# One maximum over two score banks in place of two over one each, in a decoder layer on one core

## The reference

```
x = layernorm(x + self_attention(x, W))             # one head
x = layernorm(x + cross_attention(x, ctx, ...))     # 16 heads of 64
x = layernorm(x + ffn(x))                           # two products, gates by a top-2 softmax

# cross_attention, for each batch and head:
q = x @ Wq + bq;  k = ctx @ Wk + bk;  v = ctx @ Wv + bv
att = softmax((q * scale) @ k.T)                    # 512 x 512, softmax along the keys
out = concat(att @ v) @ Wo + bo
```

## Time and profile before

| | us |
|---|---|
| median of 3 runs | 1870.48 |
| lowest and highest run | 1868.18, 1873.57 |
| the profiled execution | 1871.99 |
| its span, from the first instruction to the last | 1870.0 |

### The profile page before, as it was taken

One profiled execution on the slowest core, in us unless ns is written; L12 is line 12 of the kernel. 1 busy time (PEld: TensorE's weight loads), 2 busy tenths in 40 slices (PEclk: granted clock), 3 DMA queues, 4 the chain that ended last, 5 costly groups with the idle time before them and its releaser, 6 DMA issues.

```text
span 1870.0 us, 28844 instructions
## 1 busy us (share of the span) xinstructions
PE 1844.4 (99%) x8863; PEld 1521.2 (81%) x8863; DVE 1573.8 (84%) x3386; ACT 1159.4 (62%) x2461; POOL 1042.6 (56%) x1108
## 2 busy tenths in 40 slices
PE   9999999989999999999999999999999999999998
PEld 8888888768888888888888888888888877778887
DVE  6676666789898998989899898998989899968887
ACT  5544554467677676776777777776777777632221
POOL 2322233246667676656656566566656666756773
PEclk9999999999999999999999999999999999999999
DMA  6777787976859786585776858576585866622121
GB/s 225 276 291 278 283 301 274 317 263 189 259 161 312 215 265 221 156 266 152 252 252 193 265 164 270 180 234 219 168 259 173 252 212 184 194 96 91 60 77 68
DMA packets 200920, 400.39 MB, mean 214 GB/s; under 512 B 18112, under 2 KB 82112, under 8 KB 198592
## 3 DMA queue, kind: packets, MB, share of 16 engines
q1 hardware_dynamic: 164720, 329.08, 54.2%
q10 hardware_dynamic: 36048, 69.48, 11.2%
HBM read 211.31 MB, written 88.08 MB: 160 GB/s over the span
## 4 chain that ended last, share of the span: by engine, by line
PE 90%; DVE 5%; DMA 2%; ACT 1%; POOL 1%; issue 1%; ACTq 0%; POOLq 0%; DVEq 0%
PE a_proj L1429 17%; PE a_turned L1429 17%; PE a_av L1468 11%; PE a_score L1442 11%; PE a_proj L48 9%; PE a_proj L1852 5%; PE a_av L1852 5%; PE a_score L48 3%; PE a_av L48 3%; PE a_turned L1452 3%; PE a_proj L1452 3%; DVE all_negmax L1242 1%; DMA all_second_buffer<-x1T_scratch 1%; DVE c_squares L1298 1%; PE a_score L1827 1%; PE a_turned L624 1%
## 5 line engine op out<-in xcount | busy, mean ns | idle before, releaser
L1021 POOL TENSOR_SCALAR c_prob<-c_prob,all_rden 128x512 f32<-128x512 f32 x512 | 352.1, 695 | 496.3 <-DVE all_rden L1248 496.2
L1106 ACT ACTIVATE c_prob<-a_score,all_negmax 128x512 f32<-128x512 f32 x512 | 347.5, 684 | 195.6 <-DVE all_negmax L1242 192.5
L1242 DVE TENSOR_REDUCE all_negmax<-a_score 128x1 f32<-128x512 f32 x512 | 328.8, 684 | 92.3 <-PE a_score L1442 92.2
L1028 POOL TENSOR_TENSOR c_landing<-c_landing,c_flip_hi 128x512 fp32r<-128x512 f32 x250 | 318.4, 1295 | 2.1 <-ACT c_flip_hi L1156 2.0
L1298 DVE STREAM_TRANSPOSE c_squares<-c_prob 128x256 f32<-128x256 f32 x500 | 291.3, 621 | 1.0 <-POOL c_prob L1021 1.0
L1442 PE MATMUL a_score<-c_ks,c_qs 128*128 128x512 f32 x1024 | 277.1, 392 | 9.7 <-ACT c_prob L1106 9.0
L1442 PEld LDWEIGHTS a_score<-c_ks,c_qs 128*128 128x128 f32 x1024 | 190.1, 188 | 56.5 <-issue 8.4
L1468 PE MATMUL a_av<-c_pt,c_vs 128*128 128x512 f32 x512 | 158.3, 391 | 0.0
L343 POOL TENSOR_SCALAR s_prob<-s_prob,s_rden 128x512 f32<-128x512 f32 x32 | 22.2, 694 | 227.5 <-DVE s_rden L515 227.5
L1156 ACT CAST c_flip_hi<-c_landing 128x512 fp32r<-128x512 f32 x250 | 143.3, 625 | 1.4 <-issue 1.3
L1429 PE MATMUL a_proj<-all_third_buffer,all_first_buffer 128*128 128x512 f32 x552 | 138.2, 399 | 0.6 <-DVE c_ks L1267 0.6
(11 more groups left out here) (230 smaller groups left out, 4028.5 us busy)
## 6 DMA issues: line engine op xcount, KB each, us to landing
c_landing<-c_squares SPq DMA_DIRECT2D x500, 128.0 KB, 2.7
c_wk<-wk_scratch SPq DMA_DIRECT2D x64, 512.0 KB, 3.9
c_wq<-wq_scratch SPq DMA_DIRECT2D x64, 512.0 KB, 4.5
c_ks<-c_ks SPq DMA_DIRECT2D x128, 256.0 KB, 3.7
all_first_buffer<-ctxT_scratch ACTq DMA_DIRECT2D x60, 512.0 KB, 8.5
all_second_buffer<-x1T_scratch ACTq DMA_DIRECT2D x60, 512.0 KB, 7.2
ctxT_scratch<-s_csp SPq DMA_DIRECT2D x8, 2048.0 KB, 7.4
c_y<-y_steps_scratch SPq DMA_DIRECT2D x16, 1024.0 KB, 5.6
```

The source lines that it names most:

```text
L1021: nc.gpsimd.tensor_scalar(prob[:, n % 2, i, :], prob[:, n % 2, i, :], rden[:, n % 2, i:i + 1], 1.0, ALU.mult, ALU.mult).then_inc(p_ready, 1)
L1028: nc.gpsimd.tensor_tensor(whole, as_f32(whole), by_square(as_f32(flip_hi_part[:, k, :])), ALU.subtract).then_inc(flip_lo, 1)
L1106: nc.scalar.activation(prob[:, n % 2, i, :], spsum[:, i % 2, :], ACT.Exp, bias=negmax[:, n % 2, i:i + 1], scale=1.0, accum_out=den[:, n % ...
L1242: nc.vector.tensor_reduce(negmax[:, n % 2, i:i + 1], spsum[:, i % 2, :], AX.X, ALU.max, negate=True).then_inc(smax, 1)
```

## The change

The two reductions of a step, each over one bank, become one reduction over both. It waits for the scores of the second tile (the count on `s_mm` is one higher), writes two columns of `negmax`, and raises `smax` by 2. Nothing else is changed: the exponentials, and what they wait for, keep their code.

```diff
-    def max_tile(g, t):
+    def max_tiles(g, t):
+
         n, i = divmod(t, T)
-        dve.wait_ge(s_mm, TILES * g + t + 1)
-        nc.vector.tensor_reduce(negmax[:, n % 2, i:i + 1], spsum[:, i % 2, :], AX.X, ALU.max,
-                                negate=True).then_inc(smax, 1)
+        dve.wait_ge(s_mm, TILES * g + t + 2)
+        nc.vector.tensor_reduce(negmax[:, n % 2, i:i + 2], spsum[:, :, :], AX.X, ALU.max, negate=True).then_inc(smax, 2)
...
-            for tile in tiles:
-                max_tile(*tile)
+            if tiles:
+                max_tiles(*tiles[0])
...
-        max_tile(0, 0)
-        max_tile(0, 1)
+        max_tiles(0, 0)
         recip(0, 0)
         recip(0, 1)
         finish(PROLOGUE[5])
-        max_tile(0, 2)
-        max_tile(0, 3)
+        max_tiles(0, 2)
```

## The result

Over six runs each the kernel after took 1880.36 us (1878.60 to 1883.00) and the kernel before 1872.03 (1868.18 to 1876.14; the three runs shown at first are among them). The ratio is 1.0043 with a 95% interval of 1.0031 to 1.0055, a loss of some 8.1 us where 6.5 were forecast. The profiled execution took 1883.00 us, 2.6 above its median, with a span of 1881.0; that of before took 1871.99.

A forecast was written before the change was run, and what follows sets the result against it. TensorE was taken as the bound; front 2.4, middle 0.7 and last stretch 3.4 made 6.5 us on top of 1871.99, so 1878.5 for the profiled execution and 1877 for the median, range 1872 to 1884.

The forecast's parts named there:

- Front: First group of eight heads in the cross-attention: TensorE's waits for exponentials grow, 5 x 0.5 less 0.1, 2.4 us.
- five late ones: Front steps where VectorE comes late, both scores long there: the exponential starts 0.54 later, each paying 0.5 us.
- Middle: Long middle of the cross-attention: projections between pairs cover the delay, except at two GpSimd waits on c_landing; 0.7 us.
- the two groups without slack: Middle groups with GpSimd work of the next stage, waiting on c_landing: each wait grows by 0.38 us.
- the 0.33 us that I had left over: Middle, path of reciprocal, GpSimd and TensorE's values: slack 0.57 us, 0.24 used by the change, so nothing waits.
- Last stretch: End of the cross-attention: five waits 3.5, two near waits 0.9, last head 0.3, less 1.3 taken back; 3.4 us.
- the two that nearly waited: Last stretch: two pairs whose exponentials end shortly before their bank is needed, put at 0.45 us each, 0.9 in all.
- idle pair: Pair where VectorE waits for the first score, not quite half of 256: reduction starts 0.45 us later, TensorE loses nothing.
- Costs two: Rival, chance 0.14: the joined instruction takes 1.37 us, late waits grow and the middle's tightest path overruns; 1881.5 us.
- Faster: Rival, chance 0.04: reduction below 0.68 us frees VectorE, twelve waits at the two ends shrink by up to 0.5; 1864.5 us.
- Every pair pays: Rival, chance 0.02: the second score's 0.45 us reaches TensorE at each of 117 idle pairs, 53 us; 1923 us.
- Taken up: Rival, chance 0.26: TensorE's DMA and GpSimd waits at front and end hide more delay; some 3 us left, 1873.5 us.

The follow-up runs named there:

- the first experiment: One reduction over both banks in the middle only, two as before in the first 24 tiles and last two groups, against the kernel before: 1870.72 us, ratio 1.0000.

## Why the prediction was right, and where not

The direction and the mechanism were right; the ratio of the forecast, 1877/1870.48 = 1.0035, lies in the measured interval. The median lies 0.4 us above the forecast's own range, 1874.5 to 1880, and well inside the whole one, 1872 to 1884. Of the 3.4 us between forecast and median, 1.6 are the kernel before, whose median over six runs is that much higher than over three.

*The instruction.* Forecast 1.22 us, measured 1.221: the slope of tensor_tensor between 128 and 512 columns held for the reduction between 512 and 1024. VectorE is free after 1.13 us, as worked out, so a dropped instruction gave it 0.07. Two of 684 ns less one of 1221 make 0.147, and the overlap within the pair, 0.08 (2 x 684 ns against 1.29 us), had hidden half of it. The Trainium skill's page "VectorE: DVE Perf Modes" (section on the TRN2 errata) would give an estimated 0.125; the 0.07 that the trace had shown beforehand is what came.

*Front, 2.4 forecast.* 2.0 in the profile, and by the steps I named: five late ones paid 0.45 to 0.55 each, 2.6 together, the two where ScalarE converts a projection first paid nothing, and 0.6 were won back. The held exponential is the cause (shown by the kernel that has that wait alone). One reading was wrong: that no projection stands between the pairs of the earlier trace rows. Half a projection does, and ahead of the first wait of the stage even a whole one of 12 matmuls:

```profile
354.84 2.90 PE L1429 MATMUL a_proj<-all_second_buffer,c_wq 128*128 128x512 f32 x12
358.36 1.40 PE L1442 MATMUL a_score<-c_ks,c_qs 128*128 128x512 f32 x4 [0.61 <-ACT c_prob L1106]
...
379.96 1.66 PE L1429 MATMUL a_proj<-all_second_buffer,c_wq 128*128 128x512 f32 x6 [0.58 <-DVE c_pt L1289]
```

Of the 11 waits for an exponential in the earlier trace rows, four stand behind a whole projection, five behind half of one and two behind none. Ahead of nine of them VectorE came to the maxima of the pair waited for 2.1 to 3.7 us after their scores had started; the other two are those without a projection. In the middle there is a whole projection between all pairs, the maxima start 0.65 to 1.10 us after their scores, and the first exponential ends at least 1.27 us before the next scores.

*Middle, 0.7 forecast.* 1.1 in the profile, of it 0.8 at the two groups without slack, where 0.7 was forecast, and 0 within 2 us in the kernel with the change there alone. The profiles of kernels without the wait for the second score in the middle (the change at the ends alone, the held exponential alone) show nothing at these two steps. That the cover is limited was right as well, but the 0.33 us that I had left over were wrong: 0.42 more cost about 1 us a group. I had followed one path, by reciprocal and GpSimd to the values; the step that lost most is another, that of the output projection, where TensorE waits for GpSimd's low part of its operand and then for the exponential.

*Last stretch, 3.4 forecast: the term that was too small.* 5.3 + 1.1 = 6.4 in the profiled execution. The waits grew as forecast, 3.8 to 7.8 us against "some 7", and two of the steps paid the 1.0 that both waits together make. By steps, the five waits paid 4.1 where the sum has 3.5, the two that nearly waited 0.7 where it has 0.9, and 1.2 were won back where it takes 1.3; the scores at 1509.25 paid 0.3 that it does not have. The excess stands at the last scores and behind them, 1.4 + 1.1 us where the sum has 0.3, and there the clock fell, which the sum did not have. By the stretches shown above the falls take up to 3.5 x 0.49 = 1.7 and 4.0 x 0.43 = 1.7 us of work, 3.4 together; without them 3.0 would be left of the 6.4. Over all runs the mean granted clock was 0.9977 after (6 runs) and 0.9988 in the first set of before (23 runs); 0.0011 of 1880 us makes 2 us, an estimate and an upper one, since each run lists its clock to three digits and TensorE doesn't need all of its time. That is about the difference between 6.5 and 8.1. The bulk of the loss is there without it: the one run of after at 0.999 took 1879.17 us. That the falls come from the longer waits is argued from their place, and against it stands that falls also come without them: in five of the profiled executions the clock fell between 405 and 421 us, in two of these with no exponential held. No run kept the waits and removed the falls.

*VectorE's idle time ahead of the maxima* was to grow by 0.45 for each idle pair and fell. In the idle step shown, the reduction does start later (1.17 after the scores instead of 0.66), yet the idle time ahead of it is 0.74 instead of the 0.94 of the earlier trace rows, since VectorE came later to it. ScalarE, whose exponentials now start late, makes VectorE wait later in the step, 18.4 and 19.3 us against 3.3 each before, and this moves VectorE's arrival at the next scores. I had followed the delay to TensorE and not back to VectorE.

*The rivals.* Costs two: out by 1.221 us; by the time alone, 1881.5 against the measured 1880.36, it would have fitted as well as the forecast. Faster: out, as 0.68 us would have been needed. Every pair pays: out by the first experiment. The Trainium skill's page "Perfetto Trace Analysis" (Optimizing Tensor Performance, Matmuls) has the rule that the evacuation of one bank should overlap the matmuls of the next; here giving it up costs at the two ends, where the maxima come late or no projection stands between two pairs, and next to nothing elsewhere. Taken up: in part only. TensorE's wait for GpSimd at the end fell from 2.2 us to 0.6, a little more than the 1.3 that I had taken back, but 1.3 us of a new wait for VectorE's low part stand beside it.

*Still open.* With two instructions, the wait for the second score in the middle costs 4.3 us by its 12 runs, and with the first exponential held as well it costs nothing. The two profiles of kernels with the former show waits for transfers in different places, one of them ahead of the first changed instruction, and the profile of the kernel before has some too. So what costs these 4.3 us is not shown, nor how an exponential between two held maxima would delay a transfer. The change itself does not have this loss.

## What to carry to other kernels

Joining two instructions that evacuate two banks saves the engine little if they already overlapped, and it moves the first consumer back by the second one's duration and by the second producer's. Price it step by step by the time between that consumer's end and the next user of the bank; work that stands between is no cover by itself, where the instruction comes late. The joined form is free only where enough time is left: here in 212 pairs of 256, at no gain, as VectorE isn't the bound there. A cover of half a microsecond is soon used up, so look for the tightest step of a group on every path and not on the one that comes to mind.

## What the runs showed of the hardware

TensorE's clock can fall to half for some 3.5 us after a wait of a microsecond or two in the middle of dense work. In the kernel after it followed stands of 2.08 and 1.31 us, in the one with maxima ahead at the end one of 1.5 us; the rows show 0.51, 0.57 and 0.66 over stretches that hold such a fall, with TensorE busy for most of them. With the wait for the second score in the middle alone, it fell for nearly 7 us around a wait of 3.2 us. So a wait there can cost more than its own length.

The length of one wait does not decide. In the profiled execution of the kernel before, waits of 1.6 us at 371.64 and of 1.4 us at the end were followed by no fall; nor were waits of 1.65 and 1.64 us in the kernel after (ahead of its scores at 404.89 and 1568.83), longer than the 1.31 that one followed. With both waits and two instructions TensorE stood for 2.27 us ahead of 1637.63, and the clock was 1.00 for the 9 us behind it.

A reduction from PSUM took 419 ns over 256 columns, 684 over 512 and 1221 over 1024 in two banks, so the second bank added hardly more than its columns (537 ns for 512, against 265 for 256).
